# Three edits at the start of a four-layer float32 kernel: the small columns loaded alone and the mask in two parts, four experts of eight summed on VectorE, and layer 0 of block 0 begun ahead of block 1's last two sums

## The reference, cut to what matters

```
# layer 0: one 256x256 weight per batch row, a sum over 8 experts, masked
w_bot = einsum('bg,got->bot', cond_8, weight * mask[None])   # weight: 8 x 256 x 256
x = x + einsum('bnt,bot->bno', x, w_bot) + bias
# layer 1: expert = argmax(cond_8 row); x += down(silu(up(x)) * gate(x)), width 512
# layer 2: softmax of cond_8, top 2 experts and one shared expert,
#          x += sum of weight_e * down(gelu(gate(x)) * up(x)), width 1024 each
# layer 3: x += x @ W_base + bias + 2 * (low-rank terms of 8 experts, weighted by cond_8)
```

## Time and profile before

| What | Value |
|---|---|
| median of 3 executions | 498.41 us (498.32, 498.41, 498.89) |
| profiled execution, its own time | 498.29 us |
| its span, first to last instruction | 496.5 us |
| PE busy | 492.1 us, 99% of the span, 2172 matmul records |
| VectorE (DVE) busy | 343.5 us, 69% |
| ScalarE (ACT) busy | 261.6 us, 53% |
| GpSimd (POOL) busy | 11.0 us, 2% |
| bytes moved by DMA | 51.58 MB, mean 104 GB/s |
| DMA in the first two of 40 slices (12.4 us each) | 313 and 404 GB/s |

### The profile page before, as it was taken

The page is one execution under the profiler, slowest core; times in us unless marked ns, Lnnn a source line. Parts: engine busy times, 40 slices in busy tenths (PEclk is TensorE's granted clock), DMA queues, the critical chain, the costliest instruction groups (busy, mean ns, idle before and its releaser), DMA issues.

```text
span 496.5 us, 6551 instructions
## 1 busy us (share of the span) xinstructions
PE 492.1 (99%) x2172; PEld 406.2 (82%) x2172; DVE 343.5 (69%) x602; ACT 261.6 (53%) x416; POOL 11.0 (2%) x16
## 2 busy tenths in 40 slices
PE   8999999999999999999999999999999999999997
PEld 6788788888888888888888888888888888888886
DVE  4768896777778676866766666566575666655645
ACT  6774564566655354554664445456654555444441
POOL 0700000000000000000000000000000000000000
PEclk9999999999999999999999999999999999999999
DMA  8905332332332333233333332232333233331002
GB/s 313 404 28 194 102 96 71 97 98 89 109 105 97 98 113 97 75 96 100 100 100 99 102 107 95 81 104 73 115 106 98 68 122 97 95 97 32 2 0 85
DMA packets 20625, 51.58 MB, mean 104 GB/s; under 512 B 2801, under 2 KB 3569, under 8 KB 20593
## 3 DMA queue, kind: packets, MB, share of 16 engines
q1 hardware_dynamic: 20016, 50.13, 31.5%
q10 hardware_dynamic: 576, 1.05, 0.6%
HBM read 49.07 MB, written 2.10 MB: 103 GB/s over the span
## 4 chain that ended last, share of the span: by engine, by line
PE 98%; DMA 1%; DVE 0%; ACT 0%; issue 0%; ACTq 0%
PE acc_ps L295 10%; PE act_ps L295 10%; PE acc_ps L297 10%; PE act_ps L297 10%; PE act_ps L296 10%; PE acc_ps L296 10%; PE lin_ps L295 10%; PE lin_ps L297 10%; PE lin_ps L296 10%; PE acc_ps L385 1%; PE aux_ps L295 1%; PE aux_ps L297 1%; PE aux_ps L296 1%; DMA cols_w<-w_in 1%; PE act_ps L341 1%; PE lin_ps L344 1%
## 5 line engine op out<-in xcount | busy, mean ns | idle before, releaser
L811 DVE TENSOR_TENSOR hid<-lin_ps,act 128x512 f32<-128x512 f32 x96 | 66.4, 691 | 98.4 <-PE lin_ps L297 98.3
L800 DVE TENSOR_TENSOR w_lo<-raw,w_hi 128x384 fp32r<-128x384 f32 x220 | 122.1, 556 | 0.0
L528 ACT ACTIVATE hid_hi<-hid 128x512 fp32r<-128x512 f32 x112 | 70.8, 632 | 91.8 <-DVE hid L811 77.2
L522 ACT ACTIVATE act<-act_ps 128x512 f32<-128x512 f32 x96 | 57.3, 597 | 115.1 <-PE act_ps L297 115.1
L819 DVE TENSOR_TENSOR hid_lo<-hid,hid_hi 128x512 fp32r<-128x512 f32 x112 | 77.4, 691 | 25.8 <-ACT hid_hi L528 25.8
L508 ACT ACTIVATE w_hi<-raw 128x768 fp32r<-128x768 f32 x111 | 92.9, 837 | 0.0
L295 PE MATMUL acc_ps<-hid_hi,w_hi 128*128 128x512 f32 x224 | 87.3, 390 | 0.0
L297 PE MATMUL acc_ps<-hid_hi,w_lo 128*128 128x512 f32 x224 | 87.2, 389 | 0.0
L296 PE MATMUL acc_ps<-hid_lo,w_hi 128*128 128x512 f32 x224 | 87.1, 389 | 0.0
L295 PE MATMUL act_ps<-x_hi,w_hi 128*128 128x512 f32 x224 | 86.9, 388 | 0.0
L296 PE MATMUL act_ps<-x_lo,w_hi 128*128 128x512 f32 x224 | 86.9, 388 | 0.0
(11 more groups left out here) (122 smaller groups left out, 339.9 us busy)
## 6 DMA issues: line engine op xcount, KB each, us to landing
raw<-w_in SPq DMA_DIRECT2D x112, 384.0 KB, 3.0
out<-x SPq DMA_DIRECT2D x7, 256.0 KB, 3.7
x<-x_in SPq DMA_DIRECT2D x3, 512.0 KB, 6.6
cols_w<-w_in ACTq DMA_DIRECT2D x4, 256.0 KB, 5.2
cols_w<-w_in SPq DMA_DIRECT2D x2, 256.0 KB, 4.8
x<-x_in SPq DMA_DIRECT2D x2, 256.0 KB, 6.5
cols_w<-w_in SPq DMA_DIRECT2D x1, 288.0 KB, 3.8
mask<-mask_in SPq DMA_DIRECT2D x1, 256.0 KB, 6.2
```

Source lines behind the costliest of these rows:

```text
L522: act_e.activation(act[:, n % 2, :], act_ps[:, n % 2, :], func, bias=bias).then_inc(act_ready, 1)
L528: act_e.activation(hid_hi[:, n % 2, :], hid[:, n % 2, :], ACT.Copy).then_inc(hid_hi_ready, 1)
L800: ins = dve.tensor_tensor(w_lo[:, n % SPLIT, a:z], raw[:, n % RAW, a:z], w_hi[:, n % SPLIT, a:z].bitcast(F32), ALU.subtract)
L811: ins = dve.tensor_tensor(hid[:, n % 2, :], lin_ps[:, n % 2, :], act[:, n % 2, :], ALU.mult)
```

## The change

- `cols` is a tensor of its own (128 partitions by 64 floats, 32 KB) with a DMA of its own, the first that SyncE issues. Piece 0 then holds experts 0 and 1 of m = 0 alone. The diagonals and the routing wait for `cols_in` instead of piece 0.
- The mask is loaded in two parts of 128 KB: the part of m = 0 where the whole mask was, the part of m = 1 behind pieces 7 and 8. `mask_row0(m)` waits for its own part. SyncE issues eleven DMAs ahead of the wait for `expert_ready`, where there were nine.
- `PE_EXPERTS` is 4: for m = 0 TensorE sums experts 0 to 3, VectorE experts 4 to 7.
- TensorE's order changes. The sums for m = 1 run in the order 4, 5, 0, 1, 2, 3; then come the products hh and lh of layer 0, m = 0, for c = 0; then the sums of experts 6 and 7 for m = 1; then the other four products of m = 0 (hh and lh for c = 1, hl for both c); then the six products of m = 1 in the order they had.

```diff
-PE_EXPERTS = 5
+PE_EXPERTS = 4
...
-        cols_w0 = sb("cols_w0", [P, NCOLS + CB * E * D])
+        cols = sb("cols", [P, NCOLS])
+        w0_flat = sb("w0_flat", [P, CB * E * D])
...
-        mask_in = sem("mask_in")
+        mask_in = [sem(f"mask_in{m}") for m in range(CB)]
+        cols_in = sem("cols_in")
...
             m, first, count = W0_PIECES[q]
-            a = NCOLS + (m * E + first) * D if q else 0
-            z = NCOLS + (m * E + first + count) * D
-            queue.dma_start(cols_w0[:, a:z], w0_d[:, a:z]).then_inc(w0_in[q], 16)
+            a, z = (m * E + first) * D, (m * E + first + count) * D
+            queue.dma_start(w0_flat[:, a:z], w0_d[:, NCOLS + a:NCOLS + z]).then_inc(w0_in[q], 16)
+
+        def load_mask(queue, m):
+            queue.dma_start(w0_half(mask, m), mask_d[:, m * D:(m + 1) * D]).then_inc(mask_in[m], 16)
...
+            sp.dma_start(cols[:, :], cols_d).then_inc(cols_in, 16)
             load_w0(sp, 0)
             load_w0(sp, 2)
             load_w0(sp, 6)
-            sp.dma_start(mask[:, :], mask_d).then_inc(mask_in, 16)
+            load_mask(sp, 0)
             for c in range(CB):
                 sp.dma_start(x_part(x_flat, 0, c), x_d[0, :, c, :]).then_inc(x0_in[c], 16)
             load_w0(sp, 7)
             load_w0(sp, 8)
+            load_mask(sp, 1)
             sp.wait_ge(expert_ready, 1)
...
-            def sum_row0(m):
-
-                experts = range(PE_EXPERTS) if m == 0 else (0, 1, 4, 5, 2, 3, 6, 7)
+            def sum_row0(m, experts, first, last):
                 for g in experts:
                     if g == W0_PIECES[w0_piece(m, g)][1]:
                         pe.wait_ge(w0_in[w0_piece(m, g)], 16)
                     pe.wait_ge(diag_ready, g + 1)
-                    mm = pe.matmul(acc_ps[:, m, 0:D], diag[:, g, :], w0[:, m, g, :], start=g == 0,
-                                   stop=g == experts[-1])
-                mm.then_inc(w0_row0_done, 1)
+                    mm = pe.matmul(acc_ps[:, m, 0:D], diag[:, g, :], w0[:, m, g, :], start=first and g == experts[0],
+                                   stop=last and g == experts[-1])
+                if last:
+                    mm.then_inc(w0_row0_done, 1)
...
+            def layer0_row0(m, steps, first, last):
+
+                for kind, c in steps:
+                    a = (m * CB + c) * P
+                    if kind == "hh":
+                        pe.wait_ge(w0_hi_ready, m + 1)
+                        pe.wait_ge(x_hi_ready[0], c + 1)
+                    if kind == "hl":
+                        pe.wait_ge(x_lo_ready[0], c + 1)
+                    if kind == "lh":
+                        pe.wait_ge(w0_lo_ready, m + 1)
+                    ins = pe.matmul(aux_ps[:, m, :], (w0_lo if kind == "lh" else w0_hi)[:, a:a + P],
+                                    x_part(x0_lo if kind == "hl" else x0_hi, 0, c), start=first and (kind, c) == steps[0],
+                                    stop=last and (kind, c) == steps[-1])
+                if last:
+                    ins.then_inc(l0_done, 1)
...
-            sum_row0(0)
-            sum_row0(1)
-            layer0_row0(0)
-            layer0_row0(1)
+
+            sum_row0(0, range(PE_EXPERTS), True, True)
+            sum_row0(1, (4, 5, 0, 1, 2, 3), True, False)
+            layer0_row0(0, [("hh", 0), ("lh", 0)], True, False)
+            sum_row0(1, (6, 7), False, True)
+            layer0_row0(0, [("hh", 1), ("lh", 1), ("hl", 0), ("hl", 1)], False, True)
+            layer0_row0(1, [(kind, c) for kind in ("hh", "hl", "lh") for c in range(CB)], True, True)
...
-                act_e.wait_ge(w0_in[0], 16)
+                act_e.wait_ge(cols_in, 16)
...
-                dve.wait_ge(w0_in[0], 16)
+                dve.wait_ge(cols_in, 16)
...
             def mask_row0(m):
+                dve.wait_ge(mask_in[m], 16)
                 if m == 0:
-                    dve.wait_ge(mask_in, 16)
```

More of the change, by code:

```diff
@@ L57, in block_at, with build @@
     return BLOCKS.index((layer, row, unit))
-def build(nc, x_d, w0_d, mask_d, w1_d, b1_d, w2_d, base_d, lora_a_d, lora_b_d, out_d):
+def build(nc, x_d, cols_d, w0_d, mask_d, w1_d, b1_d, w2_d, base_d, lora_a_d, lora_b_d, out_d):
     ctx = ExitStack()
@@ L193, in build @@
         x_flat = x[:, :, :, :].rearrange("p b c t -> p (b c t)")
-        cols = cols_w0[:, 0:NCOLS]
-        w0 = cols_w0[:, NCOLS:NCOLS + CB * E * D].rearrange("p (m e d) -> p m e d", m=CB, e=E)
+        w0 = w0_flat[:, :].rearrange("p (m e d) -> p m e d", m=CB, e=E)
         def x_part(t, b, c):
@@ L1069 @@
         "x_in": arr(x).reshape(B, T, CB, P).transpose(0, 3, 2, 1),
+        "cols_in": cols,
         "w0_in": np.concatenate([cols, by_half(in_blocks(L0_cond_weight)).reshape(E, P, CB, D).transpose(
```

## The result

The changed kernel takes 500.47 us in the median of six executions (499.94 to 502.33), the kernel before 498.28 us beside it (six, 498.04 to 498.89). The ratio is 1.0042, 95% interval 1.0027 to 1.0057: 2.1 us slower. Forecast were 498.3 us and a range up to 498.9. The profiled execution is the slowest of the six, 502.33 us with a span of 500.3; the other five have spans of 498.0 to 499.0 against 496.5 before.

A forecast was written before the change was run, and what follows sets the result against it. TensorE's chain (98% of the span) bounds the kernel, so the start of `first_tiles` decides. Minus 0.43 (sum), minus 0.18 (start), plus 0.46 (products), plus 0.05 (wait) gave minus 0.1: 498.3 us, range 497.7 to 498.9.

The forecast's parts named there:

- The landing: Small columns on SyncE's queue: taken to land at 3.5 us, where piece 0 landed at 4.5 before.
- The estimate of 2.8: Columns' landing from the skill page's fixed cost of about 2.0 us; said to change nothing, ScalarE being free only at 4.1.
- Its data queue behind the same number of bytes as before. I put all this at nothing, between -0.1 and +0.1: Mask in two parts, two more SyncE issues: first `raw` tile not issued later, effect between -0.1 and +0.1 us.
- at 1.17 + 4.3 = 5.5: Piece 2's landing from issue plus transfer time: 5.5 us, the limit for VectorE's first expert operation.
- The slower rival: Start of the loads: 256-byte column rows delay pieces 0, 2 and 6 by about 0.4; 498.7 us; two slower cases together 22%.
- The test it named: VectorE's first expert operation: a start of L754 later than 5.6 us decides for the slower case.
- the new wait for the high part: Middle of TensorE's list, before the first layer 0 product: high part ready at 9.8, wait 0 to 0.1 us.
- Minus 0.43 (sum): TensorE ahead of the m = 1 sums: one sum fewer of 13, 0.43 us less.
- The order gives back what the fourth expert took: TensorE before the last m = 1 sum: two products more, 0.46 us, against one sum fewer, 0.43.
- The claim that VectorE's list and not TensorE sets `first_tiles`: Ahead of `first_tiles`: `add_x1` waits for VectorE's mask and low part, starting at 12.75 instead of 12.82.
- priced it at 0.18 us: TensorE's start 0.44 us earlier, in the half-pace stretch: worth 0.18 us if the full clock comes at the same time.
- 4% for slower by a microsecond or more: Whole kernel: chance of slower, half of the 8% for anything of a microsecond or more.

The follow-up runs named there:

- e1: Kernel before plus only the small columns as a load of their own ahead of piece 0; 499.66 us, ratio 1.0019.
- e7: Kernel before plus an unused load of one 64-byte row ahead of piece 0 on SyncE's queue; 500.07 us, ratio 1.0024.
- e10: Kernel before plus an unused load of one 64-byte row first on ScalarE's queue alone; 499.78 us, ratio 1.0028.
- e6: Kernel before plus an unused 32 KB load of 16 rows of 2048 bytes ahead of piece 0; 499.81 us, ratio 1.0031.
- e8: Kernel before with PE_EXPERTS 4 alone; 498.50 us, ratio 1.0001.
- e12: Kernel before with TensorE's new order alone, five experts on TensorE for m = 0; 498.96 us, ratio 1.0007.
- e2: Changed kernel with the small columns back in piece 0, the other edits kept; 498.93 us, ratio 1.0016.
- e3: Changed kernel with the columns' array last instead of second in HBM; 500.64 us, ratio 1.0037.
- e5: Kernel before plus an unused 32 KB load of 128 rows of 256 bytes ahead of piece 0; 500.47 us, ratio 1.0029.
- e9: Kernel before plus an unused load of one 64-byte row first on each of SyncE's and ScalarE's queues; 498.75 us, ratio 1.0008.
- e13: Kernel before with ScalarE's loads in the order 1, 4, 3, 5 instead of 1, 3, 4, 5; 498.74 us, ratio 1.0008.
- e17: Kernel before with ScalarE's four pieces read from a second copy of the weight array in HBM; 499.42 us, ratio 1.0022.
- e11: Changed kernel with the small columns split into two loads of 64 rows, one on each queue; 500.10 us, ratio 1.0033.

## Why the prediction was wrong

**The columns, and with them the loads behind.** The landing (3.3 for 3.5), the diagonals (4.02 for 4.13) and the routing were right. The estimate of 2.8 took the 2.0 us that the Trainium skill's page "DMA: Bandwidth & Descriptors" states under "Anatomy of one DMA" for the gpsimd path; the columns went by SyncE's queue and took 2.6. The step that failed is the one that carried the loads: "Its data queue behind the same number of bytes as before. I put all this at nothing, between -0.1 and +0.1", and with it piece 2 "at 1.17 + 4.3 = 5.5". Bytes ahead divided by 400 GB/s held only for the loads of the kernel before. In the changed kernel the rate was 301 and the pieces that are waited for landed 2.0 and 2.4 us late. So what had been L754 (now L761) started at 7.49, not 5.5, the addition at 9.65, not 7.7, and TensorE stood idle for 2.43 us ahead of the m = 1 sums. That one more load slows the rest is shown (e1, e7, e10); why it does is open.

**The slower rival had the sign and the place, but not the cause or the size.** It priced 0.4 us for lost rows in the slow stretch up to 3.0 us. That stretch was in fact no slower than before (273 GB/s from 2 to 3 us against 182); the loss came behind it, from 3 us on (342 against 401 GB/s from 3 to 5 us), and e6 and e7 cost as much without small rows. The test it named, L754 later than 5.6, was the right one.

**The wait in the middle of TensorE's list.** I looked only at the new wait for the high part. The one that bit is the wait for piece 6: the new order takes experts 4 and 5 of m = 1 first, hence piece 6, which now lands at 9.4, when piece 4, with experts 0 and 1, was there at 7.7. I had put piece 6 in the rows and never held its 7.0 against 7.17.

**The order against the fourth expert.** "Minus 0.43 (sum)" was mis-sized: alone it is worth 0.0 (e8), where TensorE caught up with piece 4 and VectorE's list grew. "The order gives back what the fourth expert took" was too kind: there was nothing to give back, and the order costs 0.35 (e12), both together with the mask 0.5 to 0.8 (e2). The two products took 0.54 between the sums in e2 and e3, 0.66 in e12, and not 0.46. The claim that VectorE's list and not TensorE sets `first_tiles` was right: e8 shows it.

**The clock.** I took the moment of full clock as fixed and priced it at 0.18 us. In the trace of the changed kernel an idle stretch of 2.43 us was followed by one mostly at the lower level (0.58 from 10 to 14 us); in e5's the 26 records took 7.79 us instead of 6.25. It differs from execution to execution. How much of the 2.1 us it makes is not known, as one execution of the changed kernel was traced.

**The chances.** 4% for slower by a microsecond or more rested on the belief that no load could be late by more than its share of bytes. The result lay there.

By size: the columns' load 0.95 by the ratio, 1.2 by the medians (e1); the rest 0.8 and 0.5 (e2), of which the order 0.35 (e12); together about 1.7 of the 2.1, with intervals of half a microsecond on each part.

## What to carry to other kernels

Where two queues load at once during a start that everything waits for, landing times read from a trace hold only for that pattern of issues: one 64-byte load put ahead on one queue cost 1.2 us here, one on each queue 0.4. Before an order is changed, hold every load that it waits for against the moment at which it is now wanted, above all where it takes the pieces in a new sequence. Work taken off one engine is worth nothing where that engine then reaches a load that has not landed, or another engine's list ends at the same moment. And compare data rates over a window that holds the whole of the loads: from 5 to 9 us e9 looked cured, from 1 to 9 us it was not. Where single traces disagree with medians, look at the spans of all executions first.

## What the runs showed of the hardware

- 16 DMA engines at a share of 0.94 to 1.05 moved anything from 301 to 405 GB/s in the same four microseconds, with nearly the same pieces in the queues. The busy share doesn't tell them apart; the rate does.
- Laying the 256 KB pieces out contiguously in HBM brought the rate of the kernel before from 402 down to 339 GB/s, and that of the changed kernel up from 301 to 381 (one trace each).
- The clock column of the windows reads 1.00 in the first microseconds too, where the records' pace is half: from 5 to 9 us it is 1.00 in before, with 16 records, and in e13, with 9, at nearly the same busy time. Only behind the first change that a trace holds does it tell the level, as the 0.58 above.
- The sums run at full pace from the first one at 5.0 to 5.2 us in e7, e9 and e17, and only from 10 us on in e5 and e11, behind the same warm-up of 3.6 us.
